# Local attention layers: the values product gives channels on the partitions, GpSimd divides the softmax weights, and the steps stand in a new order

## The chip, the cores and the metric

The kernel runs on one core of one Trainium2 chip. The time is device microseconds of one execution; lower is better. The core has five engines with a queue each (TensorE or PE, VectorE or DVE, ScalarE or ACT, GpSimd or POOL, SyncE or SP), a fast memory SBUF, and PSUM, eight banks of 128 partitions x 512 float32, into which TensorE writes.

## The reference, cut to what matters

The program is a two-layer network on 8 samples of 256 tokens with 128 channels. Its last stage, the only one that changes, is six layers of local attention with a feed-forward part:

```
q, k, v = split(x @ Wqkv)                     # 16 heads of 64 channels
q = l2norm(q) * qs;  k = l2norm(k) * ksc      # then rotary with a scale
# blocks of 32 queries see their own and the previous block: 64 keys
attn = softmax(where(mask, -max, q @ k.T * 8))
out = attn @ v                                # heads side by side: 1024 channels
x = x + out @ Wo
h, gate = split(layernorm(shift(x)) @ W1 + b1)
x = x + (h * gelu(gate)) @ W2 + b2
```

All of it is float32.

## The kernel before, in words

The function `local1` handles one (layer, sample) pair per iteration, 6 x 8 = 48 in all. Three iterations are in work at once: in iteration `it` the FRONT part projects sample `it`, the MID part does the attention of `it - 1`, the LATE part the output projection and feed-forward of `it - 2`. So 50 bodies run: `it` 0 and 1 written out, 2 to 47 as a loop (46 times), 48 and 49 written out.

Each engine has its own `body`, a list of steps in a fixed order written by hand. An engine takes its steps strictly in that order; where a step needs another engine's result, the engine waits there. `order` is the bank plan: it gives each product of TensorE a PSUM bank, in TensorE's order. A product may start when the reader of the bank's previous product is done (`jobs.free`), its readers wait for `jobs.filled`, and `jobs.taken` says that it has been read.

The products of an iteration (t is the half of the tokens, y is 0 for q and 1 for k; a name with two banks has .0 and .1):

- `Zty` (`project`, L2039): projection. ACT squares it (`squares`), DVE multiplies it with the rotary tables (`rotary`) and sums the squares (`square_sums`), ACT takes the root (`roots`), POOL adds the halves (`rotary_sum`) and scales (`unit`).
- `Tty` (`turn`, L2050): transposes of q and k. ACT copies them out (`turned`).
- `St` (`scores`, L2060 and L2067): mask, then 64 small products, each on a quarter of the columns of one half of the array's rows. DVE subtracts the maximum (`less_maximum`), ACT takes the exponential (`exps`), DVE sums and inverts the sum (`sums`).
- `Pt` (`turn_weights`, L2092): transposes of the weights, still undivided; ACT copies them out (`take_weights`).
- `Ot` (`values`, L2107): 64 small products per half, weights stationary (64 rows x 32 columns), values moving (64 columns); tokens come out on the partitions. DVE multiplies by the inverse sum (`by_sum`, L2483).
- `OTt` (`turn_outputs`, L2122): transposes of that result, so that channels lie on the partitions. ACT copies them out (`take_outputs`, L2285).
- `WO`, `mean`, `var`, `F0` to `F2`, `OUT2`: output projection (L2133), layer norm, feed-forward (L2159, L2168).
- `V0` to `V3` (`project_values`, L2080): projection of the values in two halves of the array's columns; ACT copies them (`take_values`, L2265). After the second half ACT raises `V_ready` and `wv_used`.

SP moves data in an order of its own. In every iteration it waits for `V_ready` and issues four DMAs that copy values to other partitions (`share_values`, L1988 and L1989). At the last sample of a layer it first waits for `wv_used`, loads the next layer's `wv`, then does `share_values`, and only then raises `front_ok` (L1974), for which TensorE waits ahead of `Z00` of the next layer. At the second sample of a layer (b = 1) it does `share_values`, then issues the loads of the feed-forward weights, and only then raises `mid_ok` (L1980), for which TensorE waits ahead of `WO` one iteration later.

Of the kernel before, what the change touches and what calls it, by code (L numbers as in the profile page):

```python
# [14 lines left out]
NT = T // 128  # L15
# [1797 lines left out]
def local1(core):  # L1813
# [3 lines left out]
    with ExitStack() as ctx:  # L1817
# [22 lines left out]
        Ot = sb("Ot3", [128, NT, H1, E1])  # L1840
# [21 lines left out]
        with nc.Block() as block:  # L1862
# [29 lines left out]
            def _(dve):  # L1892
# [4 lines left out]
                with dve.Fori(0, NB) as b:  # L1897
# [26 lines left out]
        e_ready = S("exps", NT)  # L1924
# [4 lines left out]
        order = (two(FRONT, "Z00", 7, 2) + two(MID, "T11", 5, 3) + [(LATE, "WO", 4)] + two(MID, "T10", 1, 6)  # L1929
                 + two(FRONT, "Z01", 0, 5) + [(LATE, "mean", 4)] + two(MID, "P0", 7, 2) + two(MID, "S1", 6, 1)  # L1930
                 + two(FRONT, "T00", 3, 7) + [(LATE, "var", 2)] + two(FRONT, "Z11", 0, 4) + two(MID, "O0", 3, 5)
                 + [(FRONT, "V0", 2), (FRONT, "V1", 7)] + two(FRONT, "Z10", 1, 6) + two(MID, "P1", 2, 3)
                 + [(LATE, "F0", 7), (LATE, "F1", 0), (LATE, "F2", 5)] + two(MID, "O1", 4, 2)
                 + [(FRONT, "V2", 3), (FRONT, "V3", 6)] + two(FRONT, "T01", 7, 1) + [(LATE, "OUT2", 5)]
                 + two(MID, "OT1", 3, 2) + two(FRONT, "S0", 0, 6) + two(MID, "OT0", 1, 4))
# [14 lines left out]
        with nc.Block() as block:  # L1950
# [74 lines left out]
            def _(pe):  # L2025
# [27 lines left out]
                def scores(it, t):  # L2053

                    for j in range(2):
                        pe.wait_ge(*jobs.taken(it, f"T{t}{1 - t}.{j}"))
# [27 lines left out]
                def turn_weights(it, m, t):  # L2084

                    pe.wait_ge(e_ready.sem, e_ready.at(m, t + 1))
                    for j in range(2):
                        n = f"P{t}.{j}"
                        pe.wait_ge(*jobs.free(it, n))
                        for i in range(4):  # L2090
                            pair = z[:, t, 8 * j + 2 * i:8 * j + 2 * i + 2, :].rearrange("p s k -> p (s k)")
                            last = nc.tensor.transpose(jobs.out(n)[:, i * 128:(i + 1) * 128], pair, core.ident[:, :])  # L2092
                        last.then_inc(jobs.sem_filled(n), 1)

                def values(it, m, t):
# [6 lines left out]
                    for i in range(H1):  # L2102
                        j, h = i % 2, i // 2
                        p, n = 64 * j, f"O{t}.{j}"
                        for w in range(4):
                            V = Ve if w % 2 == 0 else Vo
                            last = nc.tensor.matmul(jobs.out(n)[w * W:(w + 1) * W, h * 64:(h + 1) * 64],  # L2107
                                                    pT[p:p + 64, t, h, w * W:(w + 1) * W], V[p:p + 64, 2 * t + w // 2, h, :],
                                                    start=True, stop=True, tile_position=(p, w * W))
                        if i >= H1 - 2:  # L2110
                            last.then_inc(jobs.sem_filled(n), 1)

                def turn_outputs(it, t):

                    for j in range(2):
                        pe.wait_ge(*jobs.taken(it, f"O{t}.{j}"))
                    for j in range(2):
                        n = f"OT{t}.{j}"
                        pe.wait_ge(*jobs.free(it, n))
                        for i in range(4):  # L2120
                            pair = Ot[:, t, 8 * j + 2 * i:8 * j + 2 * i + 2, :].rearrange("p s e -> p (s e)")
                            last = nc.tensor.transpose(jobs.out(n)[:, i * 128:(i + 1) * 128], pair, core.ident[:, :])  # L2122
                        last.then_inc(jobs.sem_filled(n), 1)
# [48 lines left out]
                def body(it, front, mid, late):  # L2172
# [13 lines left out]
                    do(mid, pair("T11"), turn, m, 1, 1)  # L2186
                    do(late, ("WO",), outputs, n)
                    do(mid, pair("T10"), turn, m, 1, 0)
                    do(front, pair("Z01"), project, 0, 1)
                    do(late, ("mean",), mean, n)  # L2190
                    do(mid, pair("P0"), turn_weights, m, 0)
                    do(mid, pair("S1"), scores, 1)
                    do(front, pair("T00"), turn, it, 0, 0)
                    do(late, ("var",), variance, n)
                    do(front, pair("Z11"), project, 1, 1)
                    do(mid, pair("O0"), values, m, 0)
                    if front:
                        pe.wait_ge(values_ok, it + 1)
                    do(front, ("V0", "V1"), project_values, 0)
                    do(front, pair("Z10"), project, 1, 0)  # L2200
                    do(mid, pair("P1"), turn_weights, m, 1)
                    do(late, ("F0", "F1", "F2"), hidden, n)
                    do(mid, pair("O1"), values, m, 1)
                    do(front, ("V2", "V3"), project_values, 1)
                    do(front, pair("T01"), turn, it, 0, 1)
                    do(late, ("OUT2",), hidden_out)
                    do(mid, pair("OT1"), turn_outputs, 1)
                    do(front, pair("S0"), scores, 0)
                    do(mid, pair("OT0"), turn_outputs, 0)
# [5 lines left out]
            def _(act):  # L2215
# [62 lines left out]
                def take_outputs(it, n, t):  # L2278

                    if not_first(n):  # L2280
                        act.wait_ge(*jobs.filled(it - 1, "WO"))
                    for j in range(2):
                        name = f"OT{t}.{j}"
                        act.wait_ge(*jobs.filled(it - 1, name))
# [35 lines left out]
                def body(it, front, mid, late):  # L2320
                    m, n = it - 1, it - 2
                    if late:
                        take_outputs(it, n, 1)
                    if mid:
                        roots(m, 1, 0)
                    if late:
                        take_outputs(it, n, 0)
                    if front:
                        squares(it, 0, 0)
                    if mid:  # L2330
                        turned(it, 1, 1)
                        exps(m, 0, it - 1)
                    if front:
                        roots(it, 0, 0)
# [4 lines left out]
                    if mid:  # L2339
                        take_weights(it, m, 0)  # L2340
                    if late:
                        square_centered(it, n)
                    if front:
                        turned(it, 0, 0)
                    if late:
                        root_variance(it)
                    if front:
                        roots(it, 0, 1)
                        squares(it, 1, 1)
                    if mid:  # L2350
                        exps(m, 1, it)
                    if late:
                        affine(n)
                    if front:
                        take_values(it, 0)
                        squares(it, 1, 0)
                        act.sem_inc(qk_used, 1)
                    if mid:
                        take_weights(it, m, 1)
                    if late:  # L2360
                        gelus(it, n)
                    if front:
                        take_values(it, 1)
# [3 lines left out]
                        turned(it, 0, 1)  # L2367
                        roots(it, 1, 1)
# [4 lines left out]
            def _(pool):  # L2373
# [29 lines left out]

                def body(it, front, mid, late):
# [3 lines left out]
                    if mid:  # L2408
                        rotary_sum(m, 1, 0)
                        unit(m, 1, 1, it - 1)  # L2410
                        unit(m, 1, 0, it - 1)
                    if front:
                        rotary_sum(it, 0, 0)
                        unit(it, 0, 0, it - 1)
                        rotary_sum(it, 0, 1)
                        unit(it, 0, 1, it - 1)
                        rotary_sum(it, 1, 1)

# [4 lines left out]
            def _(dve):  # L2423
# [31 lines left out]
                def less_maximum(it, m, t, scored):  # L2455

                    ps = [jobs.out(f"S{t}.{j}").rearrange("p (h k) -> p h k", h=8) for j in range(2)]
                    if not_first(m):
# [269 lines left out]
```

## Time and profile before

| | us |
|---|---|
| median of 3 runs | 2930.97 (2927.56 to 2934.77) |
| the profiled execution | 2935.86 |
| its span | 2934.0 |

| engine | busy over the span | share |
|---|---|---|
| PE matmul | 2526.6 | 86% |
| DVE | 2117.3 | 72% |
| ACT | 1788.5 | 61% |
| POOL | 1300.1 | 44% |

The stage of the change begins at about 1275 us with the first projection and takes the rest of the span. A matmul of float32 has two records, one for each of its two passes, each with a weight load (PEld) and a stream (PE). So 64 small products of one half show as 128 records. "Busy" of a group is the time that its records cover together; the mean is the length of one, most of which is latency: the distance between starts is what a pass costs.

### The profile page before, as it was taken

To read this page: it belongs to the slowest core of one execution; us is meant where nothing else is said; L and a number is where in the kernel's file an instruction comes from. 1 tells how busy PE (TensorE), PEld (TensorE's weight loads), DVE (VectorE), ACT (ScalarE), POOL (GpSimd) and SP (SyncE) were. 2 spreads that over 40 slices of the span, in tenths; PEclk is the share of its full clock that TensorE was granted. 3 is DMA by queue.
4 is the path that set the end of the run, shared out by engine and by line. 5 is a ranking of instruction groups with operands and counts; after the bars stand their busy time and mean duration, and the time that the engine had idled before them with its cause. 6 is when DMAs were issued, how large, how long until landed. Compare 5 with 4: busy or idle time off the path is not lost. (4 is left out here: it accounts for less than half of the span.)

```text
span 2934.0 us, 95518 instructions
## 1 busy us (share of the span) xinstructions
PE 2526.6 (86%) x35932; PEld 1732.5 (59%) x35932; DVE 2117.3 (72%) x3264; ACT 1788.5 (61%) x3671; POOL 1300.1 (44%) x966
## 2 busy tenths in 40 slices
PE   5999858895637777559999999999999999999995
PEld 3777535664423333226677767777677767777674
DVE  4888643223217999648888888888888888888883
ACT  3666422333216667336777777777777777777772
POOL 1444223222123444335555555555555555555550
PEclk9999978998768999769999999999999999999997
DMA  8200015760420000011112111211211111121110
GB/s 288 66 0 0 4 31 152 219 198 24 130 70 1 0 0 0 16 49 28 25 46 52 25 25 46 52 25 25 54 39 31 46 40 25 38 54 33 25 33 20
DMA packets 124766, 149.22 MB, mean 51 GB/s; under 512 B 12016, under 2 KB 111536, under 8 KB 120240
## 3 DMA queue, kind: packets, MB, share of 16 engines
q1 hardware_dynamic: 120592, 139.81, 17.8%
q0 software_dynamic: 4096, 8.40, 1.0%
q8 instruction: 45, 0.74, 0.1%
q14 instruction: 33, 0.27, 0.0%
HBM read 76.86 MB, written 27.26 MB: 35 GB/s over the span
## 5 line engine op out<-in xcount | busy, mean ns | idle before, releaser
L2389 POOL TENSOR_TENSOR c<-a,bq 128x1024 f32<-128x1024 f32 x192 | 453.5, 2362 | 384.7 <-DVE bq L2445 384.7
L2399 POOL TENSOR_TENSOR qn<-c,ss 128x1024 f32<-128x1024 f32 x192 | 378.2, 1970 | 28.6 <-issue 7.2
L2039 PE MATMUL ps<-wqk,xs 128*128 128x512 f32 x768 | 372.6, 608 | 12.0 <-POOL xs L2382 8.7
L2224 ACT ACTIVATE sq<-ps 128x512 f32<-128x512 f32 x384 | 223.3, 594 | 96.8 <-PE ps L2039 96.7
L2444 DVE TENSOR_TENSOR a<-ps,tab 128x512 f32<-128x512 f32 x384 | 262.7, 684 | 24.2 <-ACT sq L2224 14.2
L2445 DVE TENSOR_TENSOR bq<-ps,tab 128x512 f32<-128x512 f32 x384 | 261.5, 681 | 0.0
L1445 POOL TENSOR_TENSOR hC<-hs,Cs 128x1024 f32<-128x1024 f32 x64 | 153.5, 2399 | 202.6 <-ACT Cs L1596 102.7
L2452 DVE TENSOR_REDUCE ss<-sq 128x16 f32<-128x1024 f32 x192 | 232.5, 1212 | 14.5 <-issue 14.5
L2039 PEld LDWEIGHTS ps<-wqk,xs 128*128 128x128 f32 x768 | 136.1, 193 | 150.3 <-issue 138.5
L2050 PEld LDWEIGHTS ps<-ident,qn 128*128 128x128 f32 x1536 | 173.5, 141 | 78.8 <-issue 66.3
L2050 PE MATMUL ps<-ident,qn 128*128 128x128 f32 x1536 | 206.1, 278 | 3.4 <-PEq L2032 3.4
L2080 PE MATMUL ps<-wv,xs 128*64 128x512 f32 x768 | 186.0, 605 | 3.2 <-PEq L2032 3.2
L2133 PE MATMUL ps<-oT,wo 128*128 128x256 f32 x768 | 175.5, 382 | 1.8 <-PEq L2032 1.8
L1519 PE MATMUL ps<-hC,ident 128*128 128x512 f32 x256 | 144.1, 702 | 24.5 <-POOL hC L1445 24.3
L2241 ACT ACTIVATE qT<-ps 128x512 f32<-128x512 f32 x192 | 104.3, 595 | 96.7 <-PE ps L2050 96.7
L2107 PEld LDWEIGHTS ps<-Ve,pT 64*32 64x32 f32 x6144 | 125.6, 105 | 56.5 <-issue 56.5
L1744 DVE TENSOR_TENSOR_SCAN hs<-dA,ps 128x1024 f32<-128x1024 f32 x64 | 146.4, 2287 | 14.0 <-issue 13.1
L2067 PEld LDWEIGHTS ps<-kT,qT 64*32 64x32 f32 x12288 | 127.7, 105 | 46.6 <-issue 46.6
L2133 PEld LDWEIGHTS ps<-oT,wo 128*128 128x128 f32 x768 | 143.4, 192 | 20.0 <-issue 2.2
L2265 ACT ACTIVATE Vo<-ps 128x512 f32<-128x512 f32 x192 | 114.7, 597 | 62.4 <-PE ps L2080 57.7
L2067 PE MATMUL ps<-kT,qT 64*32 64x64 f32 x12288 | 143.7, 226 | 5.6 <-issue 5.6
L2483 DVE TENSOR_TENSOR Ot<-ps,sm 128x512 f32<-128x512 f32 x192 | 123.8, 686 | 32.9 <-PE ps L2107 22.4
(309 smaller groups left out, 5864.9 us busy)
## 6 DMA issues: line engine op xcount, KB each, us to landing
Ve<-Vo SPq DMA_DIRECT2D x96, 256.0 KB, 4.3
Ve<-Vo SPq DMA_DIRECT2D x96, 192.0 KB, 4.4
win_rows<-rows_q SPq DMA_DIRECT2D x24, 256.0 KB
outs_q<-win_out SPq DMA_DIRECT2D x24, 256.0 KB
wqk<-in_wqkv SPq DMA_DIRECT2D x6, 1024.0 KB, 5.0
leaves<-in_f_w SPq DMA_DIRECT2D x9, 576.0 KB
leaves<-in_q_w SPq DMA_DIRECT2D x1, 4608.0 KB, 16.9
leaves<-in_k_w SPq DMA_DIRECT2D x1, 4608.0 KB, 22.2
```

Source lines behind the costliest of these rows:

```text
L1445: nc.gpsimd.tensor_tensor(four(hC), four(hs), spread(Cs[:, s, :], 2), ALU.mult).then_inc(hC_ready.sem, 1)
L2039: nc.tensor.matmul(jobs.out(n), xs[:, t * 128:(t + 1) * 128], wqk[:, (2 * y + s) * 512:(2 * y + s + 1) * 512], start=True, stop=True).then ...
L2050: last = nc.tensor.transpose(jobs.out(n)[:, i * 128:(i + 1) * 128], src, core.ident[:, :])
L2067: last = nc.tensor.matmul(jobs.out(n)[w * W:(w + 1) * W, m * 64:(m + 1) * 64], qT[p:p + 64, t, m, w * W:(w + 1) * W], kT[p:p + 64, even:od ...
L2080: last = nc.tensor.matmul(jobs.out(n)[p:p + 64, :], xs[:, g * 64:(g + 1) * 64], wv[:, p * 8:p * 8 + 512], start=True, stop=True, tile_posi ...
L2133: last = nc.tensor.matmul(jobs.out("WO")[:, 0:T], wo[:, i, :], oT[:, i, :], start=(i == 0), stop=(i == H1 // 2 - 1))
L2224: nc.scalar.activation(sq[:, y, :, s, :], heads_view(jobs.out(n)), ACT.Square).then_inc(sq_ready.sem, 1)
L2389: nc.gpsimd.tensor_tensor(f(c), f(a), f(bq), ALU.add).then_inc(c_ready.sem, 1)
L2399: nc.gpsimd.tensor_tensor(qn[:, t, y, :, :, :].rearrange("p h s e -> p h (s e)"), c[:, y, :, :, :].rearrange("p h s e -> p h (s e)"), spre ...
L2444: nc.vector.tensor_tensor(a[:, y, :, s, :], Zs, spread(table(0, s), H1), ALU.mult)
L2445: nc.vector.tensor_tensor(bq[:, y, :, 1 - s, :], Zs, spread(table(1, 1 - s), H1), ALU.mult)\
L2452: nc.vector.tensor_reduce(ss[:, y, :], sq[:, y, :, :, :].rearrange("p h s e -> p h (s e)"), axis=AX.X, op=ALU.add)\
```

## The change

The values product swaps its operands: the values are stationary (64 rows x 64 columns), the weights move (32 columns), and channels come out on the partitions. Head 2m+j writes bank `Ot.j`, partitions 64 x (m mod 2). The result can be used by the output projection as it is, so the transposes `OTt`, their buffer and DVE's `by_sum` go. As the sum over keys no longer lies on a partition of the result, the weights themselves are divided ahead of their transposes, by one POOL instruction per half (`by_sum` on GpSimd, 128 x 1024). `Wo` has its rows permuted to match. The score product of half 0, its exponential and its sum move from the next iteration into the same one; the order of steps on all four engines and the bank plan are new. SP's code is the same.

```diff
 # values (TensorE)
                         for w in range(4):
                             V = Ve if w % 2 == 0 else Vo
-                            last = nc.tensor.matmul(jobs.out(n)[w * W:(w + 1) * W, h * 64:(h + 1) * 64],
-                                                    pT[p:p + 64, t, h, w * W:(w + 1) * W], V[p:p + 64, 2 * t + w // 2, h, :],
-                                                    start=True, stop=True, tile_position=(p, w * W))
+                            half, at = 64 * (h % 2), (h // 2) * 128 + w * W
+                            last = nc.tensor.matmul(jobs.out(n)[half:half + 64, at:at + W], V[p:p + 64, 2 * t + w // 2, h, :],
+                                                    pT[p:p + 64, t, h, w * W:(w + 1) * W], start=True, stop=True, tile_position=(p, half))
-                def turn_outputs(it, t):
...
 # outputs (TensorE)
-                            pe.wait_ge(*jobs.taken(it - 1, f"OT{t}.{j}"))
+                            pe.wait_ge(*jobs.taken(it - 1, f"O{t}.{j}"))
 # turn_weights (TensorE)
-                    pe.wait_ge(e_ready.sem, e_ready.at(m, t + 1))
+                    pe.wait_ge(weights_ready.sem, weights_ready.at(m, t + 1))
 # body (ScalarE), its end
+                    if mid:
+                        take_outputs(it, m, 1)
+                    if front:
+                        exps(it, 0, it)
+                        roots(it, 1, 0)
                         take_values(it, 1)
                         act.drain()
                         act.sem_inc(V_ready.sem, 1)
                         act.sem_inc(wv_used, 1)
-                        turned(it, 0, 1)
-                        roots(it, 1, 1)
 # GpSimd
+                def by_sum(m, t):
+                    pool.wait_ge(sums_ready.sem, sums_ready.at(m, t + 1))
+                    nc.gpsimd.tensor_tensor(z[:, t, :, :], z[:, t, :, :], spread(sm[:, t, :], 2 * W, 2), ALU.mult).then_inc(weights_ready.sem, 1)
                     if mid:
-                        rotary_sum(m, 1, 0)
-                        unit(m, 1, 1, it - 1)
                         unit(m, 1, 0, it - 1)
+                        by_sum(m, 0)
                     if front:
                         rotary_sum(it, 0, 0)
+                        rotary_sum(it, 0, 1)
                         unit(it, 0, 0, it - 1)
-                        rotary_sum(it, 0, 1)
                         unit(it, 0, 1, it - 1)
+                    if mid:
+                        by_sum(m, 1)
+                    if front:
                         rotary_sum(it, 1, 1)
+                        unit(it, 1, 1, it)
+                        rotary_sum(it, 1, 0)
 # VectorE: by_sum goes; reciprocal in sums raises sums_ready
-                    nc.vector.reciprocal(sm[:, t, :], sm[:, t, :])
+                    nc.vector.reciprocal(sm[:, t, :], sm[:, t, :]).then_inc(sums_ready.sem, 1)
 # Wo, on the host
-    a["wo1"] = f("Wo").reshape(L1, H1 // 2, 128, D).transpose(0, 2, 1, 3).reshape(L1 * 128, H1 // 2 * D)
+    a["wo1"] = f("Wo").reshape(L1, H1 // 4, 2, 2, E1, D).transpose(0, 2, 4, 3, 1, 5).reshape(L1 * 128, H1 // 2 * D)
```

TensorE's loop body before: Z00, T11, WO, T10, Z01, mean, P0, S1, T00, var, Z11, O0, V0 V1, Z10, P1, F0 to F2, O1, V2 V3, T01, OUT2, OT1, S0, OT0. After: Z00, WO, T10, Z01, T11, P0, mean, S1, Z11, var, O0, T00, V0 V1, T01, Z10, S0, P1, F0 to F2, V2 V3, O1, OUT2.

On TensorE, the end of the loop body before, from the last projection of values (L2080) on; L2050 is `T01`, L2168 is `OUT2`, L2122 are the transposes `OTt`, L2060 and L2067 the scores:

```order
L2080 MATMUL ps<-wv,xs 64x512 x2
L2044 REGISTER_ALU
L2050 MATMUL ps<-ident,qn 128x128 x4
L2047 REGISTER_ALU
L2050 MATMUL ps<-ident,qn 128x128 x4
L2165 REGISTER_ALU
L2168 MATMUL ps<-hid,w 128x256
L2167 REGISTER_ALU
L2168 MATMUL ps<-hid,w 128x256 x2
L2116 REGISTER_ALU
L2119 REGISTER_ALU
L2122 MATMUL ps<-ident,Ot 128x128 x8
```

The same end of TensorE's body after the change: L2078 is the projection of values, L2106 the first and the last of the 64 products of `O1`, L2154 is `OUT2`:

```order
L2078 MATMUL ps<-wv,xs 64x512 x2
L2098 REGISTER_ALU x2
L2106 MATMUL ps<-pT,Ve 64x32
L2106 MATMUL ps<-pT,Vo 64x32
...
L2106 MATMUL ps<-pT,Ve 64x32
L2106 MATMUL ps<-pT,Vo 64x32
L2151 REGISTER_ALU
L2153 REGISTER_ALU
L2154 MATMUL ps<-hid,w 128x256 x3
```

`O1` stood ahead of the last values' projection, with four jobs behind `T01`; now only `OUT2` stands between it and the next iteration's `Z00`, and the transposes are gone.

On ACT, the end of the loop body before: the copies of `V2` and `V3` (L2265) follow the table load behind the gelus, with the copies of `T01` (L2247) and a root behind them:

```order
L2318 ACT_TABLE_LOAD
L2260 REGISTER_ALU
L2264 REGISTER_ALU
L2265 ACTIVATE Vo<-ps 128x512
L2264 REGISTER_ALU
L2265 ACTIVATE Vo<-ps 128x512
L2247 ACTIVATE kT<-ps 128x2x128 x2
L2239 REGISTER_ALU
L2247 ACTIVATE kT<-ps 128x2x128 x2
```

The same after the change (L2269 copies `O1`, L2239 is the exponential, L2214 and L2216 are the root, L2249 copies `V2` and `V3`):

```order
L2302 ACT_TABLE_LOAD
L2268 REGISTER_ALU
L2269 ACTIVATE oT<-ps 128x4x128
L2268 REGISTER_ALU
L2269 ACTIVATE oT<-ps 128x4x128
L2239 ACTIVATE z<-z 128x1024
L2213 REGISTER_ALU
L2214 ACTIVATE ss<-ss,eps 128x16
L2216 ACTIVATE ss<-ss,eps 128x16
L2248 REGISTER_ALU
L2249 ACTIVATE Vo<-ps 128x512
```

The copies of `V2` and `V3` moved behind the copies of `O1`, an exponential and a root.

## Rows read from the trace of the kernel before

**Rows 1.** Windows: one steady stretch; busy per engine, granted clock, DMA share, GB/s.
```profile
1400.00:2800.00 1400.00, 1400.00 (x27621) 985.90 (x27620) 1215.45 (x1910) 1066.02 (x2168) 788.72 (x553) 1.00 0.16 38
```
**Rows 2.** Line 1945, the loop's head on TensorE's queue: duration, first and last start.
```profile
L1945 PEldq FUSED_REGOPS  x46: 41/41/46, 1343.0 to 2828.2; - x46
```
**Rows 3.** Timeline of TensorE, one iteration: start, length, what.
```profile
2004.28 1.88 PE L2039 MATMUL ps<-wqk,xs 128*128 128x512 f32 x4
2006.00 1.04 PE L2050 MATMUL ps<-ident,qn 128*128 128x128 f32 x8
2006.87 3.62 PE L2133 MATMUL ps<-oT,wo 128*128 128x256 f32 x16
2010.33 1.04 PE L2050 MATMUL ps<-ident,qn 128*128 128x128 f32 x8
...
2019.34 0.24 PE L2107 MATMUL ps<-Ve,pT 64*32 64x64 f32 x1
...
2020.61 0.22 PE L2107 MATMUL ps<-Vo,pT 64*32 64x64 f32 x1
2020.76 1.94 PE L2080 MATMUL ps<-wv,xs 128*64 128x512 f32 x8
2022.62 1.98 PE L2039 MATMUL ps<-wqk,xs 128*128 128x512 f32 x4
```
**Rows 4.** Timeline of TensorE's weight loads, at half clock, at full, and in two column halves.
```profile
389.21 6.95 PEld L890 LDWEIGHTS ps<-top_w,tokens 128*128 128x128 f32 x32
...
706.13 0.53 PEld L890 LDWEIGHTS ps<-top_w,tokens 128*128 128x128 f32 x4
...
2020.76 0.20 PEld L2080 LDWEIGHTS ps<-wv,xs 128*64 128x64 f32 x4
```
**Rows 5.** Timeline of ACT, steady iteration.
```profile
2018.71 0.29 ACT L2230 ACTIVATE ss<-ss,eps 128x16 f32<-128x16 f32 x1
2019.29 1.06 ACT L2224 ACTIVATE sq<-ps 128x512 f32<-128x512 f32 x2
2020.24 1.05 ACT L2255 ACTIVATE z<-z 128x1024 f32<-128x1024 f32 x1
2021.19 0.59 ACT L2307 ACTIVATE cent<-cent,par 128x256 f32<-128x256 f32 x1
...
2034.17 1.09 ACT L2285 ACTIVATE oT<-ps 128x512 f32<-128x512 f32 x2 [0.21 <-PE ps L2122]
```
**Rows 6.** Groups by line, same stretch as rows 1: count | busy us, mean ns | idle ahead.
```profile
L2483 DVE TENSOR_TENSOR Ot<-ps,sm 128x512 f32<-128x512 f32 x170 | 109.6, 686 | 27.2 <-PE ps L2107 17.2 <-issue 10.0
...
L2399 POOL TENSOR_TENSOR qn<-c,ss 128x1024 f32<-128x1024 f32 x170 | 335.3, 1972 | 25.3 <-issue 6.6
```
**Rows 7.** Timeline of ACT: the last copies of values of iterations 7 and 9.
```profile
1800.45 0.60 ACT L2265 ACTIVATE Vo<-ps 128x512 f32<-128x512 f32 x1 [0.26 <-PE ps L2080]
...
1866.51 0.60 ACT L2265 ACTIVATE Vo<-ps 128x512 f32<-128x512 f32 x1 [0.26 <-PE ps L2080]
```
**Rows 8.** Lines 1974 (front_ok) and 1980 (mid_ok) on SP's queue, there.
```profile
L1974 SPq EVENT_SEMAPHORE  x1: 17/17/17, 1805.0 to 1805.0; - x1
...
L1980 SPq EVENT_SEMAPHORE  x1: 17/17/17, 1872.7 to 1872.7; - x1
```
**Rows 9.** Timeline of TensorE: Z00 of iteration 8, WO of iteration 10.
```profile
1806.40 1.88 PE L2039 MATMUL ps<-wqk,xs 128*128 128x512 f32 x4
...
1874.95 1.25 PE L2133 MATMUL ps<-oT,wo 128*128 128x256 f32 x5
```
**Rows 10.** Windows: a pause of TensorE, and what followed four pauses of 4 to 6 us.
```profile
452.90:457.40 4.50, 0.01 (x1) 0.00 (x0) 3.74 (x13) 0.60 (x1) 1.88 (x3) 0.66 0.50 157
457.40:461.20 3.80, 3.77 (x26) 1.91 (x26) 2.37 (x4) 0.60 (x1) 1.96 (x3) 0.50 0.12 35
578.90:584.00 5.10, 5.10 (x26) 3.18 (x26) 1.45 (x2) 0.77 (x2) 1.71 (x2) 0.50 0.97 297
646.40:652.30 5.90, 5.85 (x29) 3.94 (x29) 1.44 (x2) 0.77 (x2) 0.00 (x0) 0.50 0.07 20
720.90:724.00 3.10, 3.06 (x24) 1.61 (x25) 2.02 (x6) 0.00 (x0) 0.00 (x0) 0.50 0.00 0
```

More of the change, by code:

```diff
@@ L1923, in local1 @@
         c_ready, qn_ready = S("c", NQ, NQ), S("qn", NQ, NQ)
-        e_ready = S("exps", NT)
+        e_ready, sums_ready, weights_ready = S("exps", NT), S("sums", NT), S("weights", NT)
         squared, scaled, xm_ready, xn_ready, gl_ready = S("squared", 1), S("scaled", 1), S("xm", 1), S("xn", 1), S("gl", FC)
         two = lambda part, n, b0, b1: [(part, n + ".0", b0), (part, n + ".1", b1)]
[L1929 to L1935, printed above, removed]
+        order = (two(FRONT, "Z00", 0, 7) + [(LATE, "WO", 4)] + two(MID, "T10", 1, 0) + two(FRONT, "Z01", 5, 3) + two(MID, "T11", 0, 4)
+                 + two(MID, "P0", 7, 1) + [(LATE, "mean", 6)] + two(MID, "S1", 0, 5) + two(FRONT, "Z11", 2, 7) + [(LATE, "var", 4)]
+                 + two(MID, "O0", 6, 3) + two(FRONT, "T00", 1, 0) + [(FRONT, "V0", 6), (FRONT, "V1", 4)] + two(FRONT, "T01", 5, 7)
+                 + two(FRONT, "Z10", 3, 2) + two(FRONT, "S0", 5, 0) + two(MID, "P1", 7, 1)
+                 + [(LATE, "F0", 6), (LATE, "F1", 3), (LATE, "F2", 4), (FRONT, "V2", 1), (FRONT, "V3", 2)] + two(MID, "O1", 5, 0)
+                 + [(LATE, "OUT2", 3)])
         jobs = Jobs(core.banks, [(n, b, 1) for _, n, b in order], N + 2)
@@ L2055, in scores @@
                     for j in range(2):
-                        pe.wait_ge(*jobs.taken(it, f"T{t}{1 - t}.{j}"))
+                        pe.wait_ge(*jobs.taken(it, f"T{t}1.{j}"))
                     for j in range(2):
@@ L2339, in body @@
                     if mid:
+                        turned(it, 1, 1)
+                    if front:
+                        roots(it, 0, 0)
+                    if mid:
                         take_weights(it, m, 0)
@@ L2472, in sums @@
                     dve.drain()
-                    nc.vector.reciprocal(sm[:, t, :], sm[:, t, :])
-                def by_sum(it, m, t):
-                    dve.drain()
-                    if not_first(m):
-                        dve.wait_ge(*jobs.filled(it - 1, f"OT{t}.1"))
-                    for j in range(2):
-                        n = f"O{t}.{j}"
-                        dve.wait_ge(*jobs.filled(it, n))
-                        nc.vector.tensor_tensor(Ot[:, t, :, :].rearrange("p (m s) e -> p m s e", s=2)[:, :, j, :],
-                                                jobs.out(n).rearrange("p (h e) -> p h e", e=E1),
-                                                spread(sm[:, t, :].rearrange("p (m s) -> p m s", s=2)[:, :, j], E1, 2), ALU.mult)\
-                            .then_inc(jobs.sem_drained(n), 1)
+                    nc.vector.reciprocal(sm[:, t, :], sm[:, t, :]).then_inc(sums_ready.sem, 1)
                 def center(it, n):
@@ L2565, in body @@
                     if front:
-                        square_sums(it, 1, 0)
+                        sums(it, 0)
                 dve.sem_inc(late_Y.sem, late_Y.credit)
```

101 lines of the change are left out of this document (39 added, 62 removed).

## The prediction

> **What bounds the kernel now.** I read the busy shares by window first. Over 1400 us of the local-attention stage TensorE is busy all the time at the full clock, DVE 1215 us (87%), ACT 76%, POOL 56% [rows 1]. "Busy" alone would not prove a bound, since records overlap, so next comes the period: the loop's head passes TensorE's queue 46 times from 1343.0 to 2828.2, 33.0 us each [rows 2]. The timeline of one iteration then shows every job starting where the one before must end: four 512-column passes take 1.72 us, sixteen of 256 columns 3.46, eight transposes 0.87 (0.109 each) [rows 3]. Nothing is left to wait for: the period is the sum of TensorE's jobs. What DVE gives up is worth nothing by itself; what TensorE gives up or gains counts 1:1, and so does every wait that reaches its queue.
>
> **The change, part by part.**
>
> *Transposes of the outputs.* 16 per iteration at 0.109 us [rows 3], by those of the same shape: -1.74 us.
>
> *The values product.* Before, the 64 products of a half fill 2019.34 to 2020.76, 1.42 us until the next job: 1.27 to the last start, 0.15 to leave the tiled mode [rows 3]. Neighbours lie in eight different tiles. A pass streams 64 columns; by the transposes (128 columns, 0.107 without issue) that is 53 ns, so 128 passes over eight tiles need at least 0.85 us.
>
> After it, a pass streams 32 columns (27 ns) but its weight load has 64 columns, and there are four tiles. What does a load cost? Where only 32 columns are streamed behind loads of 128, loads follow each other by (6.95 - 0.33)/31 = 0.213 us at half clock, and by (0.53 - 0.19)/3 = 0.113 at full clock; with 64 columns the second load of a tile ends the group of four at 0.20 with 0.136 of its own length, so it starts about 0.055 after the first [rows 4]. A load costs time by its columns, 0.055 us for 64, and it is longer than the stream it hides behind. So each tile is bound by its loads: 16 products x 2 passes x 0.055 = 1.76 us per half if all four tiles work at once, plus 0.15 to leave. The catch is the order: four neighbours (w = 0 to 3) use the same tile, the next free one is four products on, the fourth twelve on. After a start with a full queue, the refill skews the tiles by some 0.15. I take 2.0 us, +0.6 per half, +1.2 per iteration.
>
> The bounds: nothing (0) if the loads overlapped better than rows 4 show; if no two tiles overlapped, 128 passes x 0.055 = 7.0, +5.6 per half.
>
> *One more change of tiling mode* (eleven per iteration for ten): the 0.15 just read, less a normal issue, +0.09.
>
> Sum of the steady iteration: -1.74 + 1.2 + 0.09 = -0.45 us, x 47 = -21 us.
>
> *POOL's division.* Two instructions of 128 x 1024, priced by `unit`'s, 1.97 us [rows 6]: POOL goes from 18.6 us of the period to 22.5 of 32.5. The chain S0, maximum, exponential, sum, division, P0 has its exponential at the end of ACT's body, 1.2 to 2.2 us after the last product of O1; sum and division (1.5 + 2.0, behind one `unit` of 2.3) are done some 7.5 us after it, and P0 stands 10 us after it. P1 waits for a sum that follows an exponential placed behind the copies of O0: by the same counting 1.3 us to spare. Both hidden; if the cover failed, 1 to 2 us per iteration.
>
> *DVE* loses four instructions of 0.64 (109.6 us in 42.5 iterations) [rows 6], worth 0, as it was not the bound.
>
> *ACT's order and the bank plan.* V0 needs the bank of O0.0, whose copy ends 0.7 after O0 while T00 takes 0.9; the next Z00 needs the bank of O1.1, whose copy ends about when OUT2 does. Zero to 0.2 us per iteration; I take 0.
>
> *The hand-over of weights, which the diff does not touch.* `V_ready` and `wv_used` rise after ACT's copies of V2, V3. Before, in iteration 7 that copy ended at 1801.05, `front_ok` rose at 1805.0, 3.9 us later, after five DMAs had been issued [rows 7, 8], and Z00 started at 1806.4: 1.4 us to spare [rows 9]. In iteration 9 the copy ended at 1867.1, `mid_ok` rose at 1872.7, 5.6 later [rows 7, 8], and WO started at 1874.95: 2.3 to spare [rows 9]. Now those copies stand behind O1. From the start E of O1's last pass: 0.2 until ACT sees it, 1.0 for the two copies, 0.95 for the exponential, 0.6 for the root, 1.1 for the copies of V2, V3 [rows 5, 7] = E + 3.85. `front_ok` comes at E + 7.75. But OUT2 (six passes of 256 columns, 1.3) is all that stands between O1 and Z00, which could start at E + 1.45: TensorE stands still 6.3 us. Two iterations later `mid_ok` comes at E + 9.45 while WO, one 1.72 behind Z00, could start at E + 3.15: again 6.3 us. Both happen five times (layers 2 to 6): 12.6 x 5 = +63 us. TensorE is the bound, so nothing is made up.
>
> Bounds: the spare times before (1.4 and 2.3) say that the margin is thin, so 0 only if my chain on ACT were 6 us too long; upwards 7 us each, 70.
>
> *The clock.* After pauses of 4 to 6 us, TensorE ran at 0.50 (1.2 GHz) for 3.8, 5.1, 5.9 and 3.1 us of dense work [rows 10], 4.5 on average, so 2.2 us lost each. Ten pauses: +22 us (0 to 30).
>
> Prologue and epilogue: the last body loses the transposes and gains sum and division ahead of P1; within 3 us of nothing.
>
> Against the profiled execution's 2935.9 (span 2934.0 and 1.9 around it): -21 + 63 + 22 = +64, so 3000. The median of the runs lies 5 lower, so **2995 us**.
>
> **A rule of the Trainium skill against the change.** The 64 small products of a half are 128 passes in 1.42 us [rows 3]. In program order the second pass of a product stands right behind its first, in the same tile, and can't start until 53 ns later; strictly in order, 64 x 53 ns = 3.4 us would be the least. So passes in other tiles overtake. The Trainium skill, "TensorE: Matmul & The Clock Gate", section "Part 3: Packing small matmuls — row/col tiling", says that matmuls are strict FIFO in start and end. The trace speaks against it here, but shows overtaking only among neighbours in different tiles; by the rule the new order would run tile after tile, which is the second rival.
>
> **The rivals.**
>
> 1. *Two of four tiles work at once*, because the overtaking reaches only some eight products ahead. For it: no row shows four neighbours in one tile. Against: the mix of passes above. 3.5 us per half instead of 1.76: a further +3.5 per iteration, x 47 = 165. About 3150.
> 2. *Tile after tile.* In a group of four, 8 passes x 0.055, the last overlapping: 5.4 to 7.0 us per half; a further +6.8 to 10 per iteration, +320 to 470: 3310 to 3460.
> 3. *The values product costs no more than before* and the pauses are shorter and cause no cold stretch: -1.65 x 47 = -78, +50 to 63: 2903 to 2916, faster by half a per cent or more. For it: streams are half as long. Against: rows 4.
> 4. *No pause at the hand-over*: copies come early enough. 2931 - 21 = 2910, faster. It decides the sign: up to 0.45 us gained in each of 47 iterations pays for two pauses per layer of 2 us each, no more. Against it: SP's code is the same and O1 stands two places from the end of TensorE's body.
>
> **How the numbers follow.** My forecast 0.58 (its own range 2955 to 3035: pauses 50 to 70, clock 0 to 30, -31 to 0 for the steady part), rival 1 0.12, rival 2 0.13, rival 3 0.10, rival 4 0.07. The range leaves out rival 2 (0.13) and the lower part of 3 and 4 (0.07): 2912 to 3180. What a measurement of this kernel tells from no change is 0.3%, 9 us: faster takes most of 3 and 4 (0.12), the same the rest of them (0.05), slower 0.83.
>
> **What would show it.** Right: no L2122 group; L2106 about 2.0 us per half, its loads longer than the 105 ns of before; a loop period of about 32.5 us in six of eight iterations; in each of layers 2 to 6 a pause of about 6 us ahead of the first Z00 and another ahead of the third iteration's WO, ended by SP, with clock 0.5 behind; POOL near 70%, never waited for by TensorE. Wrong: no SP among those TensorE waits for; L2106 at 3.5 us or more per half; TensorE waiting for POOL's division in the steady iteration; or a period below 32.

## The result, and the profile after

The changed kernel takes 3228.53 us (median of 4 runs, 3225.42 to 3236.57); before takes 2932.3 beside it (4 runs). The ratio is 1.101, 95% interval 1.0993 to 1.1031: slower by 296 us, where 64 were forecast. The forecast was 2995 us with a range of 2912 to 3180. The profiled execution took 3229.9 (span 3227.7).

First the page's groups for TensorE (out<-in, shapes, count | busy, mean ns | idle time just before, and what ended it):

```profile
L2106 PE MATMUL ps<-pT,Ve 64*64 64x32 f32 x6144 | 427.7, 225 | 1.8 <-PEq L2030 1.8
...
L2037 PE MATMUL ps<-wqk,xs 128*128 128x512 f32 x768 | 379.6, 617 | 43.7 <-SPq L1972 29.2
L2106 PEld LDWEIGHTS ps<-pT,Ve 64*64 64x64 f32 x6144 | 355.7, 134 | 56.7 <-issue 56.7
...
L2119 PE MATMUL ps<-oT,wo 128*128 128x256 f32 x768 | 187.0, 399 | 34.5 <-SPq L1978 32.3
```

No group of output transposes is left. The values product (now L2106) is TensorE's largest, and two jobs, `Z00` (L2037) and `WO` (L2119), wait for SP: 29.2 + 32.3 = 61.5 us.

Next a window of the steady stage, answering [rows 1], and what TensorE waited for in that same window (us in total, times, longest):

```profile
1500.00:2800.00 1300.00, 1250.77 (x20885) 917.42 (x20884) 881.91 (x1344) 803.57 (x1674) 725.15 (x493) 0.98 0.13 31
```

```profile
PE ps L2119 <- SPq L1978: 25.9, 4, 6.5
PE ps L2037 <- SPq L1972: 23.3, 4, 5.9
```

TensorE is idle 49.2 us of 1300, and the two SP waits are 25.9 + 23.3 = 49.2. It waits for nothing else; GpSimd is not in the list. All the rest of the loss is in jobs that take longer. The loop's head gives the period [rows 2]:

```profile
L1943 PEldq FUSED_REGOPS  x46: 41/41/46, 1336.5 to 3112.7; - x46
```

That is (3112.7 - 1336.5)/45 = 39.5 us on average. From one `mean` product to the next it is 37.55 in a steady iteration (32.98 before), and about 46 in the ten iterations with a pause. So there are two losses. From the first `mean` to the last, 47 periods, 1846.7 us pass (1549.2 before): 47 x 4.57 = 215 for the steady part, and 82 more for the pauses (84.3 in the ten iterations that have one; the stage's last two are 2.6 shorter than the rest in sum). Little lies outside these 47: the spans of the two profiled executions differ by 293.7 us, the stretches from first to last `mean` by 297.5.

**The steady part.** TensorE's timeline over one half of the values product (start, length, what), answering [rows 3]:

```profile
2005.95 0.30 PE L2106 MATMUL ps<-pT,Ve 64*64 64x32 f32 x2
...
2006.21 0.30 PE L2106 MATMUL ps<-pT,Ve 64*64 64x32 f32 x4
2006.32 0.30 PE L2106 MATMUL ps<-pT,Vo 64*64 64x32 f32 x4
2006.47 0.30 PE L2106 MATMUL ps<-pT,Ve 64*64 64x32 f32 x4
2006.58 0.30 PE L2106 MATMUL ps<-pT,Vo 64*64 64x32 f32 x4
2006.73 0.30 PE L2106 MATMUL ps<-pT,Ve 64*64 64x32 f32 x4
...
2010.22 0.28 PE L2106 MATMUL ps<-pT,Vo 64*64 64x32 f32 x2
2010.43 1.35 PE L2154 MATMUL ps<-hid,w 128*128 128x256 f32 x5
```

The half fills 2005.95 to 2010.43, 4.48 us to the next job, against 1.42 before. Every 0.26 us (2006.21, 2006.47, 2006.73) the picture repeats: that is one group of four products, the four windows of one head, all in one tile of the array. Sixteen groups make the 4.2 us. Rows of four passes mix the tail of one tile with the head of the next: the passes of two tiles overlap at a time, never of more. The passes of one tile follow each other at 0.058 us; a group has eight of them, 0.466, so a new tile starts when 4.5 of the eight pass times have gone by and 3.5 are still to come. In the weight loads, five of the eight passes have begun by then and three wait. Twice (4.48 - 1.42) is 6.12 per iteration; less the 1.74 of the transposes, that leaves +4.38 of the measured +4.57.

**The pauses.** The hand-over from the first layer to the next inside the loop, as TensorE and ACT show it [rows 5, 7]:

```profile
1880.62 0.28 PE L2106 MATMUL ps<-pT,Vo 64*64 64x32 f32 x2
1880.83 1.56 PE L2154 MATMUL ps<-hid,w 128*128 128x256 f32 x6
1888.30 3.77 PE L2037 MATMUL ps<-wqk,xs 128*128 128x512 f32 x4 [5.91 <-SPq L1972]
```

```profile
1880.68 1.08 ACT L2269 ACTIVATE oT<-ps 128x512 f32<-128x512 f32 x2 [4.14 <-PE ps L2106]
1881.65 1.06 ACT L2239 ACTIVATE z<-z 128x1024 f32<-128x1024 f32 x1
...
1883.20 1.09 ACT L2249 ACTIVATE Vo<-ps 128x512 f32<-128x512 f32 x2
```

SP's queue meanwhile (start, length, line of an issue), and the raising of `front_ok`, answering [rows 8]:

```profile
1884.55 0.34 SPq L1958 DMA_DIRECT2D wv<-in_wqkv  x1
1884.94 0.51 SPq L1986 DMA_DIRECT2D Ve<-Vo  x1
...
1886.92 1.10 SPq L1987 DMA_DIRECT2D Ve<-Vo  x1
```

```profile
L1972 SPq EVENT_SEMAPHORE  x1: 17/17/17, 1888.2 to 1888.2; - x1
```

The row of 1880.62 holds two passes; the second of them, the last of `O1`, starts at E = 1880.68. ACT has copied the values out at 1884.29 (E + 3.61), SP issues its load and four copies, `front_ok` rises at 1888.2 (E + 7.5), and `Z00` starts at 1888.30 (E + 7.62), after 5.91 us of standing still. The granted clock behind the two kinds of pause, answering [rows 10]:

```profile
1888.30:1891.80 3.50, 3.50 (x4) 1.49 (x5) 0.58 (x1) 0.60 (x1) 0.00 (x0) 0.50 0.90 191
...
1973.97:1977.00 3.03, 3.03 (x7) 2.49 (x8) 0.00 (x0) 0.00 (x0) 0.13 (x1) 0.50 0.34 114
```

`Z00`'s four passes take 3.57 us to the next job instead of 1.72: the granted clock is at 0.50, 1.2 GHz, behind the pause.

### The profile page after: what moved, and what is told of

It is laid out like the page before. It is cut to its first block and busy times, and to the rows that moved or that the text cites. A ratio compares the mean times of both kernels' runs of the same rounds, so it can differ in the third digit from the quotient of the medians.

```text
span 3227.7 us, 93440 instructions
## 1 busy us (share of the span) xinstructions
PE 2766.5 (86%) x35164; PEld 1961.4 (61%) x35164; DVE 2031.9 (63%) x3072; ACT 1758.9 (54%) x3671; POOL 1467.3 (45%) x1062
## 5 line engine op out<-in xcount | busy, mean ns | idle before, releaser
L2106 PE MATMUL ps<-pT,Ve 64*64 64x32 f32 x6144 | 427.7, 225 | 1.8 <-PEq L2030 1.8
L2106 PE MATMUL ps<-pT,Vo 64*64 64x32 f32 x6144 | 426.0, 220 | 0.0
L2037 PE MATMUL ps<-wqk,xs 128*128 128x512 f32 x768 | 379.6, 617 | 43.7 <-SPq L1972 29.2
L2106 PEld LDWEIGHTS ps<-pT,Ve 64*64 64x64 f32 x6144 | 355.7, 134 | 56.7 <-issue 56.7
L2381 POOL TENSOR_TENSOR qn<-c,ss 128x1024 f32<-128x1024 f32 x192 | 365.1, 1902 | 28.4 <-issue 3.7
L2106 PEld LDWEIGHTS ps<-pT,Vo 64*64 64x64 f32 x6144 | 356.1, 136 | 0.0
L2269 ACT ACTIVATE oT<-ps 128x512 f32<-128x512 f32 x192 | 104.2, 595 | 360.1 <-PE ps L2106 360.1
L2389 POOL TENSOR_TENSOR z<-z,sm 128x1024 f32<-128x1024 f32 x96 | 182.6, 1902 | 232.5 <-DVE sm L2464 221.8
L2037 PEld LDWEIGHTS ps<-wqk,xs 128*128 128x128 f32 x768 | 137.1, 195 | 152.1 <-issue 135.2
L2119 PE MATMUL ps<-oT,wo 128*128 128x256 f32 x768 | 187.0, 399 | 34.5 <-SPq L1978 32.3
L2502 DVE SCALAR_TENSOR_TENSOR Y<-ps,par,Y 64x256 f32 (+1 forms) x96 | 46.5, 484 | 261.1 <-PE ps L2154 260.4
L2462 DVE TENSOR_REDUCE sm<-z 128x16 f32<-128x1024 f32 x96 | 117.1, 1220 | 143.9 <-ACT z L2239 129.1
L2379 POOL TENSOR_SCALAR ss<-ss 128x16 f32<-128x16 f32 x192 | 46.9, 244 | 353.1 <-ACT ss L2216 330.6
L2119 PEld LDWEIGHTS ps<-oT,wo 128*128 128x128 f32 x768 | 155.3, 203 | 83.3 <-issue 62.4
```

Of the source, the lines that this page charges most:

```text
L2037: nc.tensor.matmul(jobs.out(n), xs[:, t * 128:(t + 1) * 128], wqk[:, (2 * y + s) * 512:(2 * y + s + 1) * 512], start=True, stop=True).then ...
L2106: last = nc.tensor.matmul(jobs.out(n)[half:half + 64, at:at + W], V[p:p + 64, 2 * t + w // 2, h, :], pT[p:p + 64, t, h, w * W:(w + 1) * W] ...
L2119: last = nc.tensor.matmul(jobs.out("WO")[:, 0:T], wo[:, i, :], oT[:, i, :], start=(i == 0), stop=(i == H1 // 2 - 1))
L2381: nc.gpsimd.tensor_tensor(qn[:, t, y, :, :, :].rearrange("p h s e -> p h (s e)"), c[:, y, :, :, :].rearrange("p h s e -> p h (s e)"), spre ...
L2389: nc.gpsimd.tensor_tensor(z[:, t, :, :], z[:, t, :, :], spread(sm[:, t, :], 2 * W, 2), ALU.mult).then_inc(weights_ready.sem, 1)
```

## The experiments

The theory that the result suggested (A): each tile of the array has a short queue of its own, room for about 3.5 pass times of work (what is left of the running pass and three that wait); TensorE hands passes out in program order and stops when the queue of the next one's tile is full. So with n products in a row in one tile, the next tile starts (2n - 3.5) x 0.058 us after the last. Two rivals: (B) the hand-out reaches a fixed number of products ahead, about eight, whatever their tiles; (C) the order doesn't matter, and it is the 64-column weight loads of which only about two tiles can have one at a time.

**e1_interleaved.** The same 64 products of a half, each neighbour in another of the four tiles. The body of the loop is the same; only the order in which it is run through changes, and with it which product of a bank is the last and signals.

```diff
-                    for i in range(H1):
-                        j, h = i % 2, i // 2
-                        for w in range(4):
+                    todo = [(j, 2 * g + s, w) for g in range(4) for w in range(4) for s in range(2) for j in range(2)]
+                    for k, (j, h, w) in enumerate(todo):
...
```

> The changed kernel with one edit: the 64 products of a half are issued so that neighbours lie in four different tiles of the array, instead of four in a row in one tile. In the changed kernel a half takes 4.48 us and a new tile starts every 0.26 us, 4.5 passes of 0.058. Theory A (each tile has a short queue of its own, some 3 to 4 passes; when it is full everything behind waits): all four tiles work, bound by their loads, 2.0 us per half; 2.45 x 2 x 47 = 230 us less, 2998 us. Rival C (no more than about two tiles can load 64-column weights at once, whatever the order): 4.4 us per half as before, 3228 us.

Measured 2994.22 us (4 runs, 2990.08 to 2996.63), ratio to before 1.0203 [1.0185, 1.0222]: 234 us of the 296 are gone through the order of the products alone. Its timeline of one half:

```profile
2006.52 0.32 PE L2105 MATMUL ps<-pT,Ve 64*64 64x32 f32 x8
2006.65 0.30 PE L2105 MATMUL ps<-pT,Vo 64*64 64x32 f32 x8
...
2008.29 0.30 PE L2105 MATMUL ps<-pT,Vo 64*64 64x32 f32 x8
2008.52 1.09 PE L2048 MATMUL ps<-ident,qn 128*128 128x128 f32 x8
```

Eight passes start every 0.117 us, where the changed kernel starts eight in 0.26; the half takes 2.00 us, the steady period is 32.59. C is out: the loads are the same ones. B is not yet told from A.

**e2_handover.** The order of products as in the changed kernel; behind the first layer, SP raises `mid_ok` and `front_ok` as soon as their own weights have landed, ahead of the four value copies.

```diff
                 def front_loaded(l):
-                    sp.wait_ge(qk_loaded, l * 16 + 16)
-                    sp.sem_inc(front_ok, NB)
+                    if type(l) is int and l == 0:
+                        sp.wait_ge(qk_loaded, l * 16 + 16)
+                        sp.sem_inc(front_ok, NB)
...
 # the same for mid_ok in rest_loaded
...
                         if b == 1 and not first:
                             sp.wait_ge(wo_used, l * NB)
                             load_mid(here)
+                            sp.wait_ge(wo_loaded, l * 16 + 16)
+                            sp.sem_inc(mid_ok, NB)
                         if b == NB - 1 and not last:
                             sp.wait_ge(qk_used, l * NB + NB)
                             load_front(there)
+                            sp.wait_ge(qk_loaded, (l + 1) * 16 + 16)
+                            sp.sem_inc(front_ok, NB)
                             sp.wait_ge(wv_used, l * NB + NB)
                             load_values(there)
```

> The changed kernel with one edit on SP: front_ok and mid_ok are raised as soon as their own weights have landed, ahead of the copies of the values, instead of behind them. The changed kernel's five iterations 7 to 8 take 45.8 us and five 9 to 10 take 46.2 instead of 37.55, 84.7 us in all. If the order on SP is the cause of the pauses and of the half clock behind them, all iterations take 37.55 us: 3144 us. Rival: the pauses come from ACT's or POOL's chain and would only move to the next wait: 3180 us or more.

Measured 3136.8 (4 runs, 3134.36 to 3142.62), ratio 1.0691 [1.0673, 1.071]: 92 us less than the changed kernel. Every period is 37.55 (the last two are shorter, as in the changed kernel), none is 46, and between 1500 and 2800 us TensorE waits for nothing. Between the profiled executions lie 87 us, 86 of them between the first and the last `mean` (1846.7 and 1760.4): the pauses and the clock behind them.

**e3_both.** Both edits.

> Both edits together, neighbours in different tiles and the early hand-over. If the two causes are separate and all there is: 3228 - 230 - 85 = 2913 us, 0.7% below the kernel before (period 32.5 us). If the tighter period uncovers another wait (POOL's division, the copies of O0 and O1): a period above 33 us and 2935 us or more.

Measured 2902.71 (4 runs, 2898.34 to 2905.41), ratio **0.9897** [0.9877, 0.9918]: the change with these two edits takes 1.0% less time than the kernel before. The two losses are separate, since e1's 234 us and e2's 92 add up to the 326 that both edits save together. A window of its steady stage, and GpSimd's division of the second half with the TensorE job that needs it:

```profile
1500.00:2800.00 1300.00, 1300.00 (x25340) 905.44 (x25339) 1070.93 (x1635) 979.24 (x2034) 882.39 (x599) 1.00 0.16 38
```

```profile
1999.73 1.90 POOL L2394 TENSOR_TENSOR z<-z,sm 128x1024 f32<-128x1024 f32 x1 [1.86 <-DVE sm L2469]
```

```profile
2003.35 1.09 PE L2096 MATMUL ps<-ident,z 128*128 128x128 f32 x8
```

TensorE is busy all the time at the full clock. The division ends at 2001.63, `P1` starts at 2003.35: 1.7 us to spare. For the first half it is 2.7 (2018.16 to 2020.87).

**e5_eights.** The changed kernel with eight products in a row in one tile: A and B differ most here.

```diff
+                    todo = [(j, 4 * g + s + 2 * v, w) for g in range(2) for s in range(2) for j in range(2) for v in range(2) for w in range(4)]
...
```

> The changed kernel with eight products in a row in one tile instead of four. Theory A (a queue per tile of some 3.5 passes): the next tile starts after 16 - 3.5 passes of 0.058 = 0.72 us, eight groups, 6.0 us per half, 1.5 x 94 = 143 us more, 3370 us. Rival B (overtaking reaches a fixed number of products ahead, about eight, so about two tiles at work in any order): 4.0 to 4.5 us per half, at most 3230 us. Rival C: 4.4 us, 3228 us.

Measured 3701.39 (one run), far above all. Two windows within one values product, the timeline in them, and a half of another iteration, whole:

```profile
2015.34:2018.60 3.26, 3.26 (x72) 3.26 (x71) 0.59 (x1) 0.19 (x1) 0.90 (x2) 1.00 0.00 0
2018.90:2023.60 4.70, 4.70 (x57) 4.70 (x56) 0.00 (x0) 0.60 (x1) 0.00 (x0) 0.50 0.00 0
```

```profile
2015.34 0.30 PE L2105 MATMUL ps<-pT,Ve 64*64 64x32 f32 x2
...
2016.06 0.30 PE L2105 MATMUL ps<-pT,Ve 64*64 64x32 f32 x4
...
2016.79 0.30 PE L2105 MATMUL ps<-pT,Ve 64*64 64x32 f32 x4
...
2017.51 0.30 PE L2105 MATMUL ps<-pT,Ve 64*64 64x32 f32 x4
```

```profile
1527.75:1533.88 6.13, 6.13 (x131) 6.09 (x129) 0.59 (x1) 0.78 (x2) 0.90 (x2) 1.00 0.00 0
```

As long as the clock is full, a new tile starts every 0.726 us (2016.064, 2016.791, 2017.517 in the trace's finer figures); A says (16 - 3.5) x 0.058 = 0.73, and a half that runs at the full clock throughout takes 6.13 us for A's 6.0 and B's 4.0 to 4.5. That settles it against B. The total, 331 us above A's 3370, was missed because of something neither theory had: in most halves the granted clock falls to 0.50 within the product, while TensorE is "busy" without a gap. The half in the first windows takes 8.35 us, and iterations 45.6 to 57. The mean granted clock is 0.843 over the span, 0.929 in the changed kernel; by an estimate from these two figures and the spans, that is some 700 us more at half clock, which can cost up to 350.

**e4_pairs** and **e6_threes.** Two in a row, and three in a row (the last round of four), otherwise as the changed kernel: two more points on A's line, without the clock's drop.

```diff
+ e4  todo = [(j, 2 * g + s, 2 * v + u) for g in range(4) for v in range(2) for s in range(2) for j in range(2) for u in range(2)]
...
+ e6  todo = sum([[(j, 2 * (k // 4) + s, k % 4) for k in range(k0, k1)]
+                 for k0, k1 in ((0, 3), (3, 6), (6, 9), (9, 12), (12, 16)) for s in range(2) for j in range(2)], [])
...
```

> The changed kernel with two products in a row in one tile. With a queue per tile of 3.5 passes the next tile may start after 2n - 3.5 passes of 0.058 for n in a row (0.26 measured for n = 4, 0.726 for n = 8): for n = 2 that is 0.03, so the four tiles' own loads are the bound, as with neighbours in different tiles: 2.0 us per half, about 2995 us. If instead every change of tile costs something fixed, or a second product in the same tile already blocks: 2.6 us or more per half, 3050 us or more.

> The changed kernel with three products in a row in one tile (a last round of four). Queue per tile: 2.5 passes of 0.058 = 0.145 us for each of sixteen groups of three, 0.26 for four of four, 3.5 us per half: 0.98 x 94 = 92 us less than the changed kernel, 3136 us. A queue counted in products (two): the group of three costs 1 product, 0.117, 3.0 us per half, 3090 us.

Measured 3007.33 and 3153.28, one run each, before 2933.29 beside them. The halves take 2.06 and 3.65 us. In e6 the first loads of new tiles stand at 2002.210, 2002.353, 2002.497 and 2002.640, 0.143 apart; A says (6 - 3.5) x 0.058 = 0.145. Distances for 3, 4 and 8 products in a row are 0.143, 0.260 and 0.726: 0.058 per further pass each time, a straight line that meets zero at 3.5 passes. With two in a row the limit is nearly gone (steady period 32.72, in e1 32.59). The whole half adds up too: in the changed kernel 16 x 0.260 + 0.32 = 4.48, in e6 16 x 0.143 + 4 x 0.260 + 0.32 = 3.65, with the same 0.32 for starting and leaving the tiled mode. The expectation for e6 had 3.5 us for a half; the 0.15 missing, 94 times, is 14 of the 17 us by which it was too low.

e4 also tells whose queue it is. Its weight loads (PEld), at the start of a half:

```profile
2010.78 0.23 PEld L2105 LDWEIGHTS ps<-pT,Ve 64*64 64x64 f32 x8 [0.33 <-issue]
2010.89 0.23 PEld L2105 LDWEIGHTS ps<-pT,Vo 64*64 64x64 f32 x8
```

In the trace's finer figures the first four loads stand at 2010.776, 2010.790, 2010.803 and 2010.816, and each opens another tile; the second load of the first tile follows at 2010.831. The streams show the same (2010.778 to 2010.818, the next at 2010.857). So the fourth tile starts 0.04 us after the first, when three of the twelve passes ahead of it in program order have begun and nine wait. A single queue for the whole array with room for 3.5 passes would have kept it waiting, and so would one for each half of the array's rows, where six passes wait (the first and the third tile share their rows). Each tile has its four passes, one begun and three waiting: as many as one tile holds in the changed kernel when the next may start. That the limit is a queue in each tile is the reading that fits all these orders; the traces show the times, not the queue.

**e7_before_fours.** The kernel before, its operands unswapped (32-column loads, 64-column streams, eight tiles), and only its products reordered so that four neighbours share a tile.

```diff
-                    for i in range(H1):
-                        j, h = i % 2, i // 2
-                        for w in range(4):
+                    todo = [(j, 4 * g + u, w) for g in range(2) for w in range(4) for j in range(2) for u in range(4)]
+                    for k, (j, h, w) in enumerate(todo):
...
```

> The kernel before with one edit: its values product, operands as they were (loads of 32 columns, streams of 64), issued with four products in a row in one of eight tiles. Queue per tile: the next tile starts after 4.5 passes of 0.056, 0.25 us, sixteen groups, 4.2 us per half instead of 1.42, 2.8 x 94 = 262 us more: 3195 us. If the limit comes from the 64-column weight loads and not from the order: no change, 2935 us.

Measured 3213.39 (one run). Its timeline:

```profile
2025.58 0.72 PE L2106 MATMUL ps<-Ve,pT 64*32 64x64 f32 x13
...
2029.32 0.69 PE L2106 MATMUL ps<-Vo,pT 64*32 64x64 f32 x13
2029.94 1.51 PE L2080 MATMUL ps<-wv,xs 128*64 128x512 f32 x6
```

4.36 us for a half instead of 1.42, 0.51 for every two groups of four; the period is 38.87 = 32.98 + 2 x 2.94 (38.86). Eight tiles help as little as four. The loss needs no swapped operands: it comes with the order. What the swap did is turn the same loop into such an order. Before, the inner index w was part of the tile's position, `(p, w * W)`, so four neighbours fell in four tiles; after it the position is `(p, half)`, w is gone from it, and four neighbours fall in one.

**e8_three_divisions.** e3_both, with GpSimd doing the second half's division twice more, into an unused buffer, ahead of the real one. It asks whether the cover read off e3's trace (1.7 us) is real.

```diff
                     pool.wait_ge(sums_ready.sem, sums_ready.at(m, t + 1))
+                    if t == 1:
+                        for _ in range(2):
+                            nc.gpsimd.tensor_tensor(spare[:, :, :], z[:, t, :, :], spread(sm[:, t, :], 2 * W, 2), ALU.mult)
+                            pool.drain()
```

> The kernel with both edits (neighbours in different tiles, early hand-over), in which POOL does the division of half 1 two more times into an unused buffer ahead of the real one. In that kernel's trace the division ends 1.7 us before TensorE reaches P1. If that is the whole cover, 3.75 us more expose 2.05 per iteration: period 34.65 us instead of 32.59, 96 us more, 3000 us. If POOL is covered all through: 2903 us. If the cover were nothing: 3080 us.

Measured 3067.47 (one run), above the forecast of 3000. The extra work on GpSimd, and TensorE behind it, in one iteration each:

```profile
2007.77 3.95 POOL L2397 TENSOR_TENSOR spare<-z,sm 128x1024 f32<-128x1024 f32 x2 [1.86 <-DVE sm L2474]
2011.86 1.90 POOL L2399 TENSOR_TENSOR z<-z,sm 128x1024 f32<-128x1024 f32 x1
```

```profile
2048.84 1.09 PE L2097 MATMUL ps<-ident,z 128*128 128x128 f32 x8 [2.36 <-POOL z L2399]
2049.77 4.44 PE L2151 MATMUL ps<-cent,w 128*128 128x256 f32 x12
```

The extra work is 2011.86 - 2007.77 = 4.09 us, and `P1` comes 2.43 later than in e3 (3.85 behind the scores product for 1.42): 1.66 were covered, as read off. The wait gives 47 x 2.43 = 114. The remainder is the clock: in every second iteration the twelve feed-forward passes behind it (L2151) take 4.37 us to the next job instead of 2.69, and the period is 36.71 instead of 35.02. That is 1.69 x 23 = 39, together 153; the trace has 155 between the first and the last `mean`. A further 10 of the 165 lies outside that stretch, where single executions differ by as much (the stage of e3 began at 1267.8 us, that of before at 1275.6). So a wait of 2.4 us costs 3.3 on average.

## Why the prediction was wrong

The direction held, and so did the mechanism of each part but one: in the values product the effect of the order was taken for a start-up effect. That mis-sized one term of the sum, by 233 us, and carried the rest out of the range.

*The failed step: "The values product", 2.0 us per half.* It measured 4.48. The price of a load was right (0.055 predicted, 0.058 measured), and so was the bound by loads: e1 reaches the 2.00 that I took for "all four tiles work at once" (1.85 to the last start and 0.15 to leave). That it is exactly 2.00 is luck: with 0.058 for a load there is nothing left for the 0.15 of skew that I had allowed. What failed is the sentence on the order, "after a start with a full queue, the refill skews the tiles by some 0.15". I saw that four neighbours use one tile and took it for a start-up effect. The runs show that passes only get past a waiting one as long as *its* tile has room, about 3.5 pass times; with eight passes in a row for one tile, the tiles behind it in program order are shut out for 4.5 of them (0.260 us), in every group anew. With this one term put right the sum is 2995 + 47 x 2 x (4.48 - 2.0) = 3228, the measured 3228.5; and with the order put right (e1) the kernel takes 2994, the predicted 2995. Agreement to a single us is partly luck: the rest of the steady period was 5 us too small in sum, and what lies outside the 47 periods was 4 us off the other way.

*Rivals 1 and 2.* Rival 1 (3150) had two tiles at work at once, which is what the trace shows; but it assumed perfect overlap of the two and put it down to a reach in products, which e5 refutes. Rival 2 (3310 and more) is the other side. Neither worked out what lies between them. Two mechanisms with the right sign and 0.25 of the chance together, and a range that ended at one of them: the price per half, which no row of before bounded between 2.0 and 5.4, should have set the top. The trace of the changed kernel shows a new tile's passes starting while 3.5 pass times of the tile ahead are still to come, and in e1 the 32 passes of each tile follow each other at 0.058 us while all 128 take 2.00; one after another they would take 7.4. By the Trainium skill ("TensorE: Matmul & The Clock Gate", "Part 3: Packing small matmuls — row/col tiling") matmuls are strict FIFO in start and end; here the starts do not keep to it across tiles: in the changed kernel the first stream of the second tile starts at 2006.214, the last three of the first tile at 2006.266, 2006.324 and 2006.383. Yet its outcome for this order (3310) was nearer to the measured time than mine (2995).

*Rival 3* (values cost no more) falls with e1: even in the best order tried they cost 2.00 against 1.42. *Rival 4* (no pause) falls with e2.

*Right:*

- TensorE as the bound and 1:1 counting: the steady period of e1 is 32.59 for 32.53 predicted (-1.74 + 1.16, and 0.19 left, which I had at 0.09 for the mode change). The timelines of one iteration place it: four jobs next to a tiled one are longer than before (`var`, `T00`, `OUT2` and `P1`, 0.34 in all), one projection is shorter by 0.09, and the transposes had taken 1.80, not 1.74.
- POOL's division hidden: in e3 1.7 and 2.7 us to spare for 1.3 and 2.5; e8 confirms the first. POOL is busy 882 us of 1300 in e3, 22.1 of 32.6.
- The hand-over: chain E + 3.61 for E + 3.85, `front_ok` at E + 7.5 for E + 7.75; pauses 61.5 us for 63. e2, which changes nothing but SP's order, has none of them.
- The clock: the ten iterations with a pause take 84.3 more than the others, less 61.5 of waits leaves 22.8, for 22 predicted.
- The 21 us gained by the steady part come back in e3: 47 x 0.39 = 18, and 20 between the first and the last `mean`. Another 7.5 lie in the stage's first iterations (69.4 us from the first projection to the first `mean`, 76.9 before), which I had at nothing and did not follow up. The remaining 5 of the 32 us are within what the start of the stage varies.

## What to carry to other kernels

When small products share the array by tiles, write the loops so that neighbours fall in different tiles, and look again when operands are swapped, since another index then picks the tile. Here two in a row were nearly free, four cost more than twice the time of the product, and no busy share showed it, since the engine counts as busy throughout. When a step is moved to the end of an engine's list, look at everything raised by the same step: here a semaphore for copied values also gated, through another queue's order, the weights of the next layer. Price a wait on the bounding engine with the slower clock behind it: here 2.3 us for each pause of about 6.

## What the runs showed that was not expected

- Passes of one tile follow each other at 0.058 us; the next tile in program order starts (2n - 3.5) x 0.058 us after the last for n products in a row: 0.143, 0.260, 0.726 us for n = 3, 4, 8. It holds with 64-column loads in four tiles; with 32-column loads in eight, e7 (n = 4) has 0.253, 4.5 passes of 0.056.
- The granted clock can fall to 0.50 with TensorE busy all the time: in e5 it does so within most of the values products, mostly 3 to 6 us after their start, while one tile, at times two, of four is at work. With four in a row no such drop appeared: in the changed kernel's steady stage the clock fell only behind a pause.
- A wait of 2.4 us per iteration was followed by a half-clock stretch in every second iteration (e8), one of 6 us every time (the changed kernel).
